# The last router stage of a fused attention and expert kernel: TensorE's order at the end, with ScalarE's and VectorE's to match

## The reference

```python
x = x + 0.5 * ffn(layernorm(x))          # first router stage
x = x + attn(layernorm(x))               # 32 heads, chunks of 128 tokens, a running state
x = x + 0.5 * ffn(layernorm(x))          # last router stage

def ffn(flat):                           # E = 64 experts, top 8
    logits = flat @ router_weight.T + router_bias
    scores = softmax(logits)
    topk_w, topk_idx = top_k(scores, 8)
    w_dense = zeros(T, E).at[arange(T)[:, None], topk_idx].add(topk_w)
    return flat * topk_w.sum(-1) + w_dense @ expert_bias
```

## Time and profile before

| | |
|---|---|
| median of 3 runs | 1636.06 us (1635.18 to 1636.61) |
| the profiled execution's own time | 1634.31 us |
| its span in the trace | 1632.5 us |
| TensorE busy | 1587.2 us, 97% of the span |
| VectorE, ScalarE, GpSimd busy | 1368.7, 1093.5, 1412.8 us |
| granted clock of TensorE, mean | 0.99 |

### The profile page before, as it was taken

One profiled execution on the slowest core, in us unless ns is written; L12 is line 12 of the kernel. 1 busy time (PEld: TensorE's weight loads), 2 busy tenths in 40 slices (PEclk: granted clock), 3 DMA queues, 4 the chain that ended last, 5 costly groups with the idle time before them and its releaser, 6 DMA issues.

```text
span 1632.5 us, 33589 instructions
## 1 busy us (share of the span) xinstructions
PE 1587.2 (97%) x11028; PEld 885.4 (54%) x11028; DVE 1368.7 (84%) x2945; ACT 1093.5 (67%) x2987; POOL 1412.8 (87%) x1316
## 2 busy tenths in 40 slices
PE   7898999999999999999999999999999999999986
PEld 6554555555555555555555555555555555555554
DVE  7988788888879888797879888887888878788976
ACT  5666676676766667766766667666676767676653
POOL 5777899888988999888988999888998989888964
PEclk8999999999999999999999999999999999999998
DMA  6022233232343224231532223222332224222222
GB/s 223 28 56 67 59 74 85 65 73 53 79 85 78 53 59 107 50 85 46 92 83 62 63 66 87 72 72 53 86 84 59 72 46 105 65 65 58 48 46 104
DMA packets 208012, 118.76 MB, mean 73 GB/s; under 512 B 173792, under 2 KB 174816, under 8 KB 206816
## 3 DMA queue, kind: packets, MB, share of 16 engines
q1 hardware_dynamic: 207840, 116.63, 30.0%
HBM read 70.19 MB, written 4.46 MB: 46 GB/s over the span
## 4 chain that ended last, share of the span: by engine, by line
PE 74%; POOL 13%; DVE 7%; issue 4%; ACT 2%; ACTq 0%; POOLq 0%; DVEq 0%
PE B L323 24%; PE B L325 23%; PE B L324 23%; POOL ROWS L1428 2%; POOL QS L1415 2%; POOL RR L1461 2%; POOL PL L1450 1%; POOL WVL L1446 1%; DVE WL L1701 1%; POOL ZS L1454 1%; POOL RM L1458 1%; POOL WVF L1438 1%; POOL K L1422 1%; PE B L553 1%; DVE PF L1645 1%
## 5 line engine op out<-in xcount | busy, mean ns | idle before, releaser
L323 PE MATMUL B<-WH,XTH 128*128 128x128 bf16 (+1 forms) x992 | 270.0, 297 | 5.0 <-DVE VL L1630 4.3
L324 PE MATMUL B<-WL,XTH 128*128 128x128 bf16 (+1 forms) x992 | 269.8, 297 | 0.0
L325 PE MATMUL B<-WH,XTL 128*128 128x128 bf16 (+1 forms) x992 | 269.8, 297 | 0.0
L1415 POOL TENSOR_TENSOR QS<-QS,SIN 128x512 f32<-128x512 f32 x160 | 219.5, 1372 | 33.6 <-ACT QS L1142 33.0
L323 PE MATMUL B<-XTH,WH 128*128 128x512 bf16 x640 | 243.3, 380 | 1.1 <-DVE G L1635 1.1
L325 PE MATMUL B<-XTH,WL 128*128 128x512 bf16 x640 | 243.3, 380 | 0.0
L324 PE MATMUL B<-XTL,WH 128*128 128x512 bf16 x640 | 243.1, 380 | 0.0
L1694 DVE SCALAR_TENSOR_TENSOR YF<-B,RR,G 128x128 f32<-128x128 f32 x512 | 144.1, 344 | 113.4 <-POOL RR L1461 113.3
L1174 ACT ACTIVATE PF<-ROWS,NG 128x128 f32<-128x128 f32 x512 | 162.8, 390 | 79.3 <-POOL ROWS L1428 78.9
L1454 POOL TENSOR_TENSOR ZS<-YF,ZS 128x512 bf16<-128x512 f32 x128 | 158.0, 1235 | 64.4 <-ACT ZS L1212 64.2
L1428 POOL TENSOR_TENSOR ROWS<-ROWS,AFTER 128x512 f32<-128x512 f32 x128 | 190.1, 1485 | 2.5 <-DMA ROWS<-rows_dram 2.5
(11 more groups left out here) (209 smaller groups left out, 4319.8 us busy)
## 6 DMA issues: line engine op xcount, KB each, us to landing
ROWS<-rows_dram SPq DMA_DIRECT2D x128, 256.0 KB, 3.2
STAGE<-in_wall SPq DMA_DIRECT2D x108, 256.0 KB, 2.8
ACC<-in_x SPq DMA_DIRECT2D x3, 1024.0 KB, 9.1
out<-ACC SPq DMA_DIRECT2D x3, 1024.0 KB, 3.9
ZT<-ZS SPq DMA_TRANSPOSE x128, 3.1
ACC<-in_x SPq DMA_DIRECT2D x4, 256.0 KB, 3.7
COS<-in_cos SPq DMA_DIRECT2D x1, 1024.0 KB, 12.8
SIN<-in_sin SPq DMA_DIRECT2D x1, 1024.0 KB, 14.8
```

Source lines behind the costliest of these rows:

```text
L323: nc.tensor.matmul(out_, ah, bh, start=first, stop=False)
L324: nc.tensor.matmul(out_, ah, bl, start=False, stop=False)
L325: return nc.tensor.matmul(out_, al, bh, start=False, stop=last)
L1415: nc.gpsimd.tensor_tensor(QS[:, sl, :], QS[:, sl, :], SIN[:, t0:t0 + TB], ALU.mult).then_inc(sin_ready.sem, 1)
```

## The change

The instructions are the same ones; their order, two banks and a few waits are other ones:

- TensorE computes the logits of the second block in two halves, chunks 0 and 1 ahead of the first block's weights and chunks 2 and 3 behind them; both stood behind the first block's mix. The product of chunk 15 follows the mix directly and waits no more for `f_acc`.
- The first block's mix of its chunks 2 and 3 goes to banks 2 and 6 (it used 1 and 3), and waits until ScalarE has read the second block's transposes from them. The third block's transposes use banks 2 and 6 as well, and its first two now wait for `f_acc` of the first block's chunks 2 and 3.
- ScalarE copies the third block's first two transposed chunks (`act_turned(NB + 2, (0, 1))`) ahead of the exponentials of the second block, not behind.
- VectorE takes the statistics of the third block's chunks in steps 13, 14 and 15 of the last group, ahead of `gated` in the first two of them, and in the last ahead of the first block's `dve_logits`; all four stood behind the first block's `dve_mixed`.
- VectorE takes the second block's `dve_logits` ahead of the first block's `dve_mixed`, and adds the product of chunk 15 ahead of the second block's `dve_choose`, not behind its `dve_weigh`.

```diff
--- before.py
+++ after.py
@@ -173,7 +173,7 @@
             return BANK[7] if f > NB and f % 2 else BANK[0]
 
         def mix(f, i):
-            return BANK[(4, 5)[i % 2] if f < NB else (5, 4, 1, 3)[i]]
+            return BANK[(4, 5)[i % 2] if f < NB else (5, 4, 2, 6)[i] if f == NB else (5, 4, 1, 3)[i]]
 
         def shared(f):
             return f in (NB + 1, NB + 2)
@@ -522,6 +522,8 @@
                     pe.wait_ge(st_ready.sem, st_ready.at(KVH - 1, cs_event(NCH - 2)))
                 elif f > NB:
                     pe.wait_ge(f_xnt.sem, f_xnt.at(f, i - 2))
+                if f == NB + 2 and i < 2:
+                    pe.wait_ge(f_acc.sem, acc_at(NB, i + 2))
                 for k in range(KT):
                     ins = nc.tensor.transpose(turned(f, i)[:, k * P:(k + 1) * P], A[:, i, k * P:(k + 1) * P], IDF[:, :])
                 ins.then_inc(f_tp.sem, 1)
@@ -633,9 +635,9 @@
                 pe.wait_ge(z_ready.sem, z_ready.at(KVH - 1, NCH - 1))
             for i in chunks:
                 if f == NB and i >= 2:
-                    pe.wait_ge(out_free.sem, out_free.at(KVH - 1, (NCH - 2, NCH - 3)[i - 2]))
-                elif f == NB + 1 and i == BLK - 1:
-                    pe.wait_ge(out_free.sem, out_free.at(KVH - 1, NCH - 1))
+                    pe.wait_ge(f_xnt.sem, f_xnt.at(NB + 1, i))
+                elif f == NB + 1 and i >= 2:
+                    pe.wait_ge(out_free.sem, out_free.at(KVH - 1, NCH - 4 + i))
                 elif f > NB + 1 and i >= 2:
                     pe.wait_ge(f_part.sem, 2 * (f - NB - 2) + i - 1)
                 elif f > NB:
@@ -1095,10 +1097,10 @@
             for n in steps(True):
                 step(KVH - 1, n, True)
             project_out(KVH - 1, NCH - 2, True)
+            pe_logits(pe, NB + 1, (0, 1))
             pe_weights(pe, NB)
+            pe_logits(pe, NB + 1, (2, 3))
             pe_mix(pe, NB)
-            pe_logits(pe, NB + 1)
-            pe.wait_ge(f_acc.sem, acc_at(NB, BLK - 1))
             project_out(KVH - 1, NCH - 1, True)
             pe_turn(pe, NB + 2)
             pe_weights(pe, NB + 1)
@@ -1384,8 +1386,9 @@
             act_exp(act, NB)
             act_turned(act, NB + 1, (2, 3))
             act_weights(act, NB)
+            act_turned(act, NB + 2, (0, 1))
             act_exp(act, NB + 1)
-            act_turned(act, NB + 2)
+            act_turned(act, NB + 2, (2, 3))
             act_weights(act, NB + 1)
             act_turned(act, NB + 3, (0, 1))
             act_exp(act, NB + 2)
@@ -1851,6 +1854,8 @@
                     dve_stats(dve, 0, NB, (n - BLK - 2,))
                 if last and 2 * BLK + 2 <= n < 3 * BLK:
                     dve_stats(dve, 0, NB + 1, (2 * (n - 2 * BLK - 2), 2 * (n - 2 * BLK - 2) + 1))
+                if last and n >= NCH - 3:
+                    dve_stats(dve, 0, NB + 2, ((0, 1), (2,), (3,))[n - NCH + 3])
                 if last and n == NCH - 1:
                     dve_logits(dve, NB)
                     add_out(g, NCH - 3, True)
@@ -1881,12 +1886,11 @@
             dve_choose(dve, NB)
             dve_weigh(dve, NB)
             add_out(KVH - 1, NCH - 2, True)
+            dve_logits(dve, NB + 1)
             dve_mixed(dve, NB)
-            dve_stats(dve, 0, NB + 2)
-            dve_logits(dve, NB + 1)
+            add_out(KVH - 1, NCH - 1, True)
             dve_choose(dve, NB + 1)
             dve_weigh(dve, NB + 1)
-            add_out(KVH - 1, NCH - 1, True)
             dve_stats(dve, 0, NB + 3)
             dve_logits(dve, NB + 2)
             dve_choose(dve, NB + 2)
```

## The result

| | before | changed |
|---|---|---|
| median of 12 runs | 1635.06 us | 1637.38 us |
| lowest and highest | 1631.66, 1636.61 us | 1633.43, 1641.24 us |
| profiled execution's own time, span | 1634.31, 1632.5 us | 1633.43, 1631.2 us |

The ratio is 1.0018, interval 1.0009 to 1.0026: the changed kernel is slower by 2.3 us in the medians (2.6 in the means), where 0.2 us less was forecast, from a median of three runs (1636.06 us) that the twelve runs put at 1635.06.

The account below looks back on a forecast made before the run. The kernel's end was taken to hang on a chain of waits through VectorE, ScalarE, GpSimd and TensorE from 1570 us on. Median 1636.06 - 1.4 (shorter chain) + 1.2 (new clock fall) gave 1635.8 us, range 1632.9 to 1637.8.

Parts of the forecast that it names:

- The half logits: TensorE, ahead of the first block's weights: 16 of the second block's 32 logits matmuls, 1.84 us, in the old wait.
- the first gate: VectorE, before the first block's weights: moved statistics make this gate 0.55 us later, bounds 0.4 to 0.95.
- the four additions: VectorE, behind the second block's logits: 2.8 us for four beside GpSimd's residual, bounds 2.7 and 3.2.
- the mix and product: TensorE, behind the second half of the logits: mix 1.73 us at full clock, product of chunk 15 ends 3.4 us earlier.
- two copies held the exponentials: ScalarE, second block: exponentials wait behind two third-block copies until 1598.7 against 1600.08, so 5.6 us gained become 1.4.
- a wait of 2.04 us: TensorE, between the third block's transposes and the second block's weights: a pause of 2.3 us where before it was 0.64.
- The chain to the third block's logits: TensorE's start of the third block's logits: 1601.9 against 1603.31, 1.4 us earlier, bounds 0.9 and 2.0.
- the size of the new fall: Third block's logits on TensorE: clock falls from 1.00 to 0.50 behind the new pause, costing 1.2 us, bounds 0 and 1.7.
- It hurt nothing there, since VectorE was later: First block's mix in the kernel before: the clock fall from 1590 on, 1.7 us of TensorE's work, cost the chain nothing.
- The clock holds: Rival at the new pause ahead of the second weights: no fall through the 2.3 us, 1634.65 us; chance 0.32.
- Faster by twice as much: Rival: clock holds and the later fall at the third block's mix is missed, saving 1.7 more, 1632.95 us; chance 0.11.
- Slower: one more fall, earlier: Rival: TensorE's pause from 1589.5 to 1590.5 brings a fall over half logits, mix and product 15; 1638.1 us; chance 0.12.

Follow-up runs that it names:

- two variants: Changed kernel with exponentials ahead of all copies, ratio 1.0004; kernel before with only the third block's first two copies ahead of the second block's exponentials, ratio 1.0027.
- the kernel of 1.0003: Changed kernel with nine bf16 dummy matmuls of 128x512 in TensorE's new wait ahead of the second block's weights: 1634.17 us against 1633.53 before, ratio 1.0003.
- the kernel with exponentials first: Changed kernel, but ScalarE makes the second block's exponentials ahead of all four copies of the third block: 1633.94 us, ratio 1.0004 against before.
- the kernel with the long f32 filling: Changed kernel with 16 f32 matmuls of 128x64 (3.68 us) in the wait of 2.04 us ahead of the second block's weights: ratio 1.0003 against before.
- the first filling: Kernel before with only TensorE's wait of 2.21 us ahead of the first block's weights filled, by nine bf16 matmuls: 1633.56 us against 1634.89, ratio 0.9992.

## Why the prediction was wrong

**Right, by its own steps.** The half logits stand in the old wait; the first gate came 0.52 us later (12.69 to 13.21 us behind the start of the first block's logits; 0.55 was predicted); the four additions took 2.72 (2.8); the mix and product ran at the full clock; two copies held the exponentials, and a wait of 2.04 us (2.3) stood ahead of the second weights. All times are 1.6 to 1.9 us earlier than predicted, 1.6 of it because this execution reached the stage 1.6 earlier. The chain to the third block's logits was shorter by 1.71 (1.4, bounds 0.9 and 2.0).

**The step that failed is the size of the new fall.** "I take 1.2 us for it, bounds 0 (no fall) and 1.7." The fall came, at the place named, but 1.7 was what the fall at 1590 lost, which lasted 3.4 us and lay over mixes; this one lasted 6.8 us, lost 3.41 and cost 2.3 on the chain, in both profiles of the changed kernel. In two variants it lasted 10.2 us and cost 32.67 - 28.9 = 3.8 and 32.87 - 28.9 = 4.0. With 2.3 for 1.2 the sum gives 1636.06 - 1.4 + 2.3 = 1637.0, and the measured median is 1637.38. That nearness is partly luck, since before's own median in the twelve runs was 1635.06. As a difference the mended sum says 0.9 us slower, and 2.3 were measured. Of the 1.4 that are missing, 0.3 are the time outside the span, for which the sum had no term; the rest is taken up under "What is less sure".

**A false statement about before.** "It hurt nothing there, since VectorE was later." It cost 1.05 us: VectorE's additions waited for the slow mix, and its second logits stood behind them. So most of what I put down to the order (1.05 of 1.71) was the clock, which did not fall there behind the shorter wait; the order's own worth is 0.67. The chain's sum came out near all the same, because it reckoned the new mix at the full clock and took the old times from a trace with a slow one: the 1.05 stands in its 1.4 without a name.

**The rivals.** "The clock holds" happens, but rarely in what was seen: one of three profiles with an unfilled wait of 2.04 us in the changed order, and filled by hand it is the kernel of 1.0003. "Faster by twice as much" rested on 1.7 us for the late fall; it was missed in the profiled execution, and is worth 29.19 - 28.9 = 0.3 at most. "Slower: one more fall, earlier" is real in some executions: behind 1.03 us in the kernel with exponentials first, and behind 1.02 in the kernel with the long f32 filling, where the clock was 0.89 in the microsecond from 1592 and 0.50 at 1595. That is two of the seven profiles in which this wait is not filled. Its price was not 1.7 both times: in the first the fall lasted 6.8 us and the first stretch is 28.30, 3.3 longer than the 24.97 of the same order filled; in the second it lasted 3.4, and the third block's transposes begin 22.73 us behind the first block's logits for 21.05 in the changed kernel, 1.7 later. So its weight of 0.12 was too low, and my argument against it (the wait is cut to about 1 us) is refuted.

**The page.** The Trainium skill, "TensorE: Matmul & The Clock Gate", section "HAM oscillation — how this bites in real kernels", has a longer pause than any of these as the condition of cooling; the runs disagree again, by falls behind 2.04, 1.21 and 1.03 us.

**What is less sure.** The changed kernel was 2.6 us slower in the means, and 1.8 when it was timed again. Its two profiles account for 0.3 in the stretches and 0.3 outside the span. Filling only the new wait gave no change against before (1.0003), though its profile's stretches are 2.0 us shorter; 0.3 of that go outside the span. Filling the other waits too brought 2.8 us in the changed order (mean differences of +0.2 and -2.6 against before), but in the kernel before only 1.3 on top of the first filling (-1.2 and -2.5), about what the fall in step 14 costs there on average. What points to a cause in both is the fall behind the wait of 1.02 us: seen in two of seven profiles, at 3.3 and 1.7 us, it would cost 0.7 us on average, an estimate. No profile of these two kernels caught it, so this is argued and not shown. With it some 1.3 us of the 2.6, and 0.5 of the 1.8, are still without a cause, and the filled new wait should have brought 1.0 us where the interval of its ratio (0.9993 to 1.0012) ends at 1.1. Nor is it known why falls differ in length.

## What to carry to other kernels

When a reordering moves idle time of TensorE, look at what work stands behind each new wait: a fall behind a wait of 1 to 2 us, ahead of work on the chain, cost more (2.3 to 4.0 us) than the order had gained. Price a clock fall with its possible length, not with the shortest one seen, and by what stands on the chain behind it. Before reordering at all, try dummy matmuls in the waits: here they gave 2.5 us without any new order, and 3.7 in the changed order with the exponentials first. And take more than one profile of each kernel: the same wait had a fall behind it in some executions and none in others.

## What the runs showed of the hardware that was not expected

- Falls of the granted clock to 0.50 came behind waits of TensorE of 2.2, 2.12, 2.04, 1.21, 1.03 and 1.02 us. Not each wait has one in each execution: behind 2.12 us the clock fell in eight of eleven profiles, behind 2.04 in three of four, behind 1.02 or 1.03 in two of seven.
- Falls lasted 3.4, 6.8, 10.2 and 13.6 us in these traces, and the clock stayed low even while TensorE was busy without a gap (1602 to 1608 in the changed kernel).
- f32 logits of 128x64 run at 0.115 us an instruction at the full clock and 0.22 at half (7.03 / 32), and as filling they kept the clock as 128x512 bf16 did.
- The time follows the mean granted clock of a run: before took 1636.3 us at 0.988, 1633.5 at 0.990 and 1631.2 at 0.992, as means of its runs beside the experiments.
- One fall of 3.4 us cost 1.7 us of the chain in step 14, 1.05 over the first block's mix and 0.3 at most over the third block's.
